# Reading the gathered distance tables one unit further ahead in a disentangled-attention stage

## The reference, cut to what matters

```
pos_k  = (rel_embeddings @ Wk + bk)                          # 128 relative positions, by head
scores = q @ k.T / scale                                     # scale = sqrt(16 * 3)
c2p    = take_along_axis(q @ pos_k.T, clip(rel + 64))        # query against position
p2c    = take_along_axis(k @ pos_k.T, clip(-rel + 64)).T     # key against position
probs  = softmax(scores + (c2p + p2c) / scale)
ctx    = probs @ v
out    = layernorm(ctx @ Wo + bo + hidden) ...
```

## Time and profile before

| | us |
|---|---|
| median of the 3 runs shown | 2644.16 |
| the profiled execution, whole | 2643.83 |
| its span, first to last instruction | 2642.1 |
| stage 1, to the barrier's end | 0 to 157 |
| stage 2, until stage 3 starts | 157 to 1369 |
| stretch between first unit and the last reads of stage 2 | 182 to 1343 |

### The profile page before, as it was taken

How to read it: one execution, slowest core, us unless ns; L and a number is a source line. 1 busy time by engine, 2 the same in 40 slices (tenths; PEclk the granted TensorE clock), 3 DMA queues, 4 the chain that set the end, 5 groups by cost and what they waited for, 6 DMA issues and landing times. The chain is left out here.

```text
span 2642.1 us, 47030 instructions
## 1 busy us (share of the span) xinstructions
PE 1935.7 (73%) x13556; PEld 1436.8 (54%) x13557; DVE 1632.1 (62%) x3986; ACT 998.6 (38%) x2034; POOL 896.3 (34%) x1082
## 2 busy tenths in 40 slices
PE   6867777777777777777759999775623438999962
PEld 3436666665566666666646666543423417887631
DVE  8946666666656666666666455258775794444444
ACT  3445555555555555555523233243201103333100
POOL 3112222222222222223222222037753005555576
PEclk9978899889989899888979999887766558999976
DMA  4579999998999999999952110000000144446544
GB/s 147 184 231 281 281 282 275 270 277 267 288 265 288 269 287 282 272 288 278 291 166 84 48 48 32 1 0 0 1 0 30 37 191 138 153 156 145 121 131 122
DMA packets 289512, 456.38 MB, mean 173 GB/s; under 512 B 38465, under 2 KB 224369, under 8 KB 289297
## 3 DMA queue, kind: packets, MB, share of 16 engines
q1 hardware_dynamic: 272688, 410.29, 50.9%
q0 software_dynamic: 16608, 43.44, 6.7%
HBM read 236.65 MB, written 216.92 MB: 172 GB/s over the span
## 5 line engine op out<-in xcount | busy, mean ns | idle before, releaser
L947 DVE CUSTOM_DVE_ANT_0 probs<-bank,c2p 128x512 f32<-128x512 f32 x512 | 351.7, 687 | 427.6 <-PE bank L844 214.8
L905 ACT ACTIVATE probs<-probs,neg_max 128x512 f32<-128x512 f32 x512 | 371.3, 725 | 68.4 <-DVE neg_max L947 68.1
L920 ACT COPY a_stage<-bank 128x320 f32<-128x320 f32 (+1 forms) x512 | 211.8, 414 | 427.9 <-PE bank L813 417.0
L956 DVE COPY probsT<-bank 128x512 f32<-128x512 f32 x512 | 351.2, 686 | 10.5 <-PE bank L854 9.9
L854 PE MATMUL bank<-ident,probs 128*128 128x128 f32 x2048 | 334.5, 289 | 3.4 <-ACT probs L905 3.3
L825 PE MATMUL bank<-tab,k 96*128 96x320 bf16 (+1 forms) x512 | 164.2, 321 | 187.3 <-DVE b_stage L899 143.3
L854 PEld LDWEIGHTS bank<-ident,probs 128*128 128x128 f32 x2048 | 277.1, 152 | 15.1 <-issue 3.8
L774 POOL COPY end_c2p<-a_stage 128x4 f32<-128x4 f32 (+1 forms) x128 | 24.7, 193 | 745.9 <-ACT a_stage L920 593.1
L2144 POOL DMA_INDIRECT p_x_tile<-y_d,p_token x160 | 152.0, 950 | 283.2 <-POOLq L1845 162.6
L844 PE MATMUL bank<-ident,p2c 128*128 128x128 f32 x1280 | 246.8, 294 | 0.0
L839 PE MATMUL bank<-k,q 96*128 96x384 bf16 (+1 forms) x512 | 166.0, 324 | 101.6 <-DMA p2c<-p2c_d 67.4
(11 more groups left out here) (265 smaller groups left out, 3700.2 us busy)
## 6 DMA issues: line engine op xcount, KB each, us to landing
p2c_d<-b_stage SPq DMA_DIRECT2D x64, 640.0 KB, 4.8
c2p_d<-a_stage SPq DMA_DIRECT2D x64, 640.0 KB
p2c_d<-b_stage SPq DMA_DIRECT2D x64, 576.0 KB, 5.1
c2p_d<-a_stage SPq DMA_DIRECT2D x64, 576.0 KB
p2c<-p2c_d SPq DMA_DIRECT2D x256, 144.0 KB, 4.3
c2p<-c2p_d SPq DMA_DIRECT2D x256, 144.0 KB, 4.1
o_sorted_d<-p_o_pair SPq DMA_DIRECT2D x80, 256.0 KB, 2.3
k<-k_stack_d SPq DMA_DIRECT2D x192, 64.0 KB
```

Source lines behind the costliest of these rows:

```text
L905: act.activation(probs[:, w % 2, j, :], probs[:, w % 2, j, :], ACT.Exp, bias=neg_max[:, w % 2, j:j + 1], scale=-1.0).then_inc(exp_done, 1)
L920: act.copy(staged(a_stage, wa % 2, wa % TPB)[:, j, :], bank[A_BANK][:, 0:width(wa % TPB)]).then_inc(a_copied, 1)
L947: dve.tensor_tensor_reduce(probs[:, w % 2, j, :], bank[S_BANKS[(HB * w + j) % 3]][:], c2p[:, w % 2, j, :], -SCALE, LOWEST, ALU.add, ALU.mi ...
L956: dve.tensor_copy(probsT[:, wp % 2, j], bank[T_BANKS[j % 2]][:].rearrange("p (k q) -> p k q", k=TPB)).then_inc(probsT_copied, 1)
```

## The change

The write leads become 4 and 5, the query side is read back two units ahead (`C2P_LEAD`) and the key side three (`P2C_LEAD`). `p2c` and both HBM tables have eight slots, `c2p` has four, and `probs` is gone: VectorE and ScalarE work in place in `c2p`'s slot. SP waits for the scores of unit n-2 and no longer for the read of a table slot before it writes it again. The prologue has five steps, not four. The quarters of a group's stacks are loaded in the first three steps of each four (two, one, one, none). The values are written to HBM by head in stage 1, with one column of ones (`v_d`), and loaded by SP, one DMA for a head. In `v_h` a tile takes 17 columns, and the matmul still reads 32, the rest of them the next tile's.

```diff
-        c2p_d = dram("c2p_d", [4, P * (B // 2) * TABLE], F32)
-        p2c_d = dram("p2c_d", [4, P * (B // 2) * TABLE], F32)
+        c2p_d = dram("c2p_d", [2 * TPB, P * (B // 2) * TABLE], F32)
+        p2c_d = dram("p2c_d", [2 * TPB, P * (B // 2) * TABLE], F32)
+        v_d = dram("v_d", [H, P, TILES, D + 1], F32)
...
                         if u:
+                            tiles = slice((b - 1) * TPB, (b + 1) * TPB)
+                            sp.wait_ge(v_ones_set, 1)
+                            sp.wait_ge(v_ready, 2 * b + 2)
+                            sp.dma_start(v_d.rearrange("h p t d -> p h t d")[:, :, tiles], v_all[:, :, tiles, :]
+                                         ).then_inc(v_stored, 16)
                             sp.wait_ge(far_split, b // 2 + 1)
...
+                    pool.memset(v_all[:, :, :, D], 1.0).then_inc(v_ones_set, 1)
+                    pool.wait_ge(v_ones_set, 1)
...
-                        dve.tensor_tensor(v_all[:, b * TPB + 2 * j:b * TPB + 2 * j + 2, :],
-                                          bank[V_BANK][:].rearrange("p (s c) -> p s c", s=2), bv_row[:], ALU.add
-                                          ).then_inc(v_ready, 1)
+                        dve.tensor_tensor(v_all[:, :, tiles, 0:D].rearrange("p h s d -> p s h d"),
+                                          bank[V_BANK][:].rearrange("p (s h d) -> p s h d", s=2, h=H),
+                                          bv_row[:].rearrange("p s (h d) -> p s h d", h=H), ALU.add).then_inc(v_ready, 1)
...
-        A_LEAD, B_LEAD = 3, 4
+        A_LEAD, B_LEAD, C2P_LEAD, P2C_LEAD = 4, 5, 2, 3
...
-            v_h = sb(st, "v_h", [P, 2, TILES, MV])
+            v_h = sb(st, "v_h", [P, 2, TILES * (D + 1) + MV - D - 1])
...
-            c2p = sb(st, "c2p", [P, 2, HB, S])
+            c2p = sb(st, "c2p", [P, 4, HB, S])
...
-            p2c = sb(st, "p2c", [P, TPB, HB, NEAR])
-            probs = sb(st, "probs", [P, 2, HB, S])
+            p2c = sb(st, "p2c", [P, 2 * TPB, HB, NEAR])
...
+                    def load_v(h, par):
+                        sp.dma_start(v_h[:, par, 0:TILES * (D + 1)],
+                                     v_d[ds(h, 1)].rearrange("h p t d -> (h p) (t d)")).then_inc(v_loaded[par], 16)
...
                         if is_unit(i, w):
-                            wait_count(sp, scores_made, HB * n)
+                            wait_count(sp, scores_made, HB * (n - 1))
                             apart(sp)
-                        (i2, w2), (i1, w1) = ahead(i, w, 2), ahead(i, w, 1)
+                        (i3, w3), (i2, w2) = ahead(i, w, P2C_LEAD), ahead(i, w, C2P_LEAD)
+                        if is_unit(i3, w3):
+                            kt = w3 % TPB
+                            sp.wait_ge(b_written[w3 % 2], 16 * (BODY // 2 * i3 + w3 // 2 + 1))
+                            apart(sp)
+                            sp.wait_ge(p2c_filled, BODY * i3 + w3 + 1)
+                            read_skewed(p2c_d, w3 % (2 * TPB), kt, p2c[:, w3 % (2 * TPB)], 0, p2c_loaded[kt])
                         if is_unit(i2, w2):
...
-                        if is_unit(i1, w1):
-                            t = w1 % TPB
-                            sp.wait_ge(a_written[w1 % 2], 16 * (BODY // 2 * i1 + w1 // 2 + 1))
-                            apart(sp)
-                            sp.wait_ge(c2p_filled, BODY * i1 + w1 + 1)
-                            read_skewed(c2p_d, w1 % 4, t, c2p[:, w1 % 2], (t - 1) * P, c2p_loaded[w1 % 2])
+                            sp.wait_ge(c2p_filled, BODY * i2 + w2 + 1)
+                            read_skewed(c2p_d, w2 % (2 * TPB), t, c2p[:, w2 % 4], (t - 1) * P, c2p_loaded[w2 % 4])
                         if is_unit(i, w) and is_unit(*ahead(i, w, 2 * TPB)):
                             slot = (w // TPB + 2) % 4
-                            load_quarter(sp, w % TPB, 2 * i + w // 8 + 1, (w // TPB) % 2, slot, group_loaded[slot])
...
+                            for r in ((0, 1), (2,), (3,), ())[w % TPB]:
+                                load_quarter(sp, r, 2 * i + w // 8 + 1, (w // TPB) % 2, slot, group_loaded[slot])
...
+                        if w % 8 == 2 and is_unit(i, w) and is_unit(*ahead(i, w, 6)):
+                            wait_count(sp, pv_made, n - 2)
+                            apart(sp)
+                            load_v(2 * i + w // 8 + 1, 1 - w // 8)
...
-                            wait_count(sp, p2c_loaded[wb % TPB], 64 * (4 * ib + wb // TPB))
...
-                    def copy_v(h, par):
-                        pool.tensor_copy(v_h[:, par, :, 0:D], v_all[:, :, ds(h * D, D)]).then_inc(v_copied, 1)
...
-                            wait_count(pool, scores_made, HB * n)
-                            pool.wait_ge(b_ends_copied, BODY * i2 + w2 + 1)
+                        if is_unit(i3, w3):
+                            t = w3 % TPB
+                            if is_unit(i, w):
+                                wait_count(pool, scores_made, HB * (n - 1))
+                            pool.wait_ge(b_ends_copied, BODY * i3 + w3 + 1)
...
-                            wait_count(pool, scores_added, HB * n)
-                            pool.wait_ge(a_ends_copied, BODY * i1 + w1 + 1)
+                            if is_unit(i, w):
+                                wait_count(pool, probs_transposed, HB * (n - 1))
+                            pool.wait_ge(a_ends_copied, BODY * i2 + w2 + 1)
...
-                    pool.memset(v_h[:, :, :, D:MV], 1.0).then_inc(ones_set, 1)
-                    copy_v(0, 0)
+                    pool.memset(v_h[:, :, TILES * (D + 1):], 0.0).then_inc(pad_set, 1)
...
-                                                probs[:, w % 2, j, kt * P:(kt + 1) * P], ident[:])
+                                                c2p[:, w % 4, j, kt * P:(kt + 1) * P], ident[:])
...
-                                pe.wait_ge(v_copied, 2 * i + g // 2 + 1)
+                                pe.wait_ge(v_loaded[g // 2], 16 * (i + 1))
...
-                                    dve.wait_ge(c2p_loaded[w % 2], 64 * (8 * i + w // 2 + 1))
+                                    dve.wait_ge(c2p_loaded[w % 4], 64 * (4 * i + w // 4 + 1))
```

## The result

The changed kernel took 2689.6 us (median of 4 runs, 2687.4 to 2694.8) against 2647.6 us for the one before (4 runs, 2642.0 to 2651.9): ratio 1.0163, interval 1.0135 to 1.0191. The forecast was 2593 us in a range of 2553 to 2640, so the sign was wrong as well as the size. In the profiled execution the span is 2686.5 us against 2642.1. Where the runs of a kernel fall into a faster and a slower state, as those of e14_stacks_by_act further down do, its ratio takes the faster ones alone.

A forecast was written before the change was run, and what follows sets the result against it. The prediction took the DMA engines to bound the attention stage, at share 0.94 and 278 GB/s. 2643.8 less 51 us there, plus 0 for the start and end, gave 2593 us, range 2553 to 2640.

The forecast's parts named there:

- The order of the group's quarters: Attention stage: bunching stack loads only shifts SP's issue time between steps; taken as nothing, up to 30 us for the range.
- SP's and POOL's waits: Attention stage: the dropped or moved waits of SP and POOL, and POOL's 16 fewer copies, change nothing; 0 us.
- One step more between read and use: Attention stage: earlier reads remove the query-side wait, 182.2 us, and most of the key-side 61.3 us; DMA queue is late next.
- The cap by the DMA engines: Attention stage: 327 MB at 300 GB/s plus 20 us of loop returns, 1110 us against 1161, a gain of 51.
- C: Attention stage: SP's own issue order is the clock; gain of 0 to 25 us, 2619 to 2644; chance 0.15.
- A: Attention stage, the forecast case: waits go and the DMA engines cap the gain; 2575 to 2615 us; chance 0.62.
- rival B: Attention stage: DMA ceiling higher than seen; at 312 GB/s a gain of 93 us, 2551; far end compute-bound; chance 0.12.
- Values by DMA: Attention stage: loading values by DMA adds 4.2 MB, making 327 MB in all, priced at 300 GB/s.
- Stage 1 and the prologue: Stage 1 +2 us, fifth prologue step +3, smaller first memset -1, last unit's read wait -4; together 0.
- Rival D: Attention stage: the DMA queue is full already, so the kernel gets slower; 2661 to 2671 us; chance 0.11.

The follow-up runs named there:

- e14_stacks_by_act: e13_act_two_bodies with the key stacks issued by ScalarE too; 0.9479 of the kernel before, from two of its four runs.
- e1_k_alone: Changed kernel with separate semaphores for key and query stacks, so the key-side product waits for the key stacks only; 0.9900 of the kernel before.
- e2_quarters_early: Changed kernel with the stack quarters loaded one a step, starting two steps earlier; 0.9899 of the kernel before.
- e9_both: The mended kernel: changed kernel with separate key and query stack semaphores and quarters one a step, two steps earlier; 0.9872 of the kernel before.
- e12_before_by_act: Kernel before with the query stacks' loads issued by ScalarE instead of SP, one step earlier; 0.9936 of the kernel before.
- e8_query_side_alone: Kernel before with query side read two units ahead into four slots, quarters two steps earlier, key side and values unchanged; 0.9944 of the kernel before.
- e10_queries_by_act: e9_both with the query stacks' loads issued by ScalarE at the end of its step instead of SP; 0.9626 of the kernel before.
- e4_before_bunched: Kernel before with only the quarters' order changed to two, one, one, none, leads as before; 1.0033 of the kernel before.
- after_again: The changed kernel unaltered, timed again on another chip beside e9_both; 1.0169 of the kernel before.
- e6_two_bodies: e9_both with two bodies in each pass of the hardware loop, two returns for five; 0.9820 of the kernel before.
- e13_act_two_bodies: e9_both with query stacks issued by ScalarE and two bodies in each loop pass; 0.9549 of the kernel before, 2525.3 us.

## Why the prediction was wrong

**The step that failed** is "The order of the group's quarters", together with "SP's and POOL's waits". It priced the new order by what its issues cost SP and took nothing for it, with 30 us as the bound. It never asked when the stack is wanted. The key-side product of a group's first unit is made `B_LEAD` units ahead; with `B_LEAD` 5 it is made in the step w % 4 = 3 of the group before, and the last quarter of the query stack is issued in the step just before that, w % 4 = 2, behind that step's eight reads. In the kernel before the distance was one step as well (quarter issued in step 3, wanted in step 0), and the prediction had its sign in hand: TensorE's 25.6 us for `q_stack`, at most 2.1 us at a time. It was read as a small wait. In its place the runs showed 255.3 us in pieces of 8.5: by the reading above, a wait with a cover, VectorE's wait for the query side, which the change takes away. The price was 71 to 78 us (e1_k_alone, e2_quarters_early, e9_both), more than all the gain that was forecast.

**"One step more between read and use"** was right in itself: 182.2 us fell to 2.3, and in the mended kernels the waits went to the staging buffers as foreseen. e12_before_by_act agrees that the lead held the kernel before. e8_query_side_alone adds that it takes both leads: the query side's alone gave 0.6%.

**The cap by the DMA engines** was too generous for this change and is not the cap that it was taken for. The prediction had a gain of 51 us in the stage, at a share of nearly 1.00 but for the returns. From the first sum to the last, e9_both takes 1137 us where the kernel before takes 1172: a gain of 35. Its share stayed at 0.96, with SP almost never waiting, so the limit of one queue that issues everything came first; the prediction gave that rival, C, a chance of 0.15 by the earlier trace rows, and took it and A as alternatives. The rate of 300 GB/s at full share is about right (309 at 1.02, 317 at 1.03), but a share of 1.00 is no ceiling even over a whole stage: e10_queries_by_act makes the same transfers in a stretch of 1069 us (180.4 to 1249.1), 103 less than before and more than rival B's 93.

**Values by DMA** were put at the bytes' price, 4.2 MB / 300 GB/s = 14 us, with about 2 us in stage 1. Alone they cost 0.41% or 11 us (6 to 16): the sum agrees, but the trace of that run shows the attention stage as long as before, so the agreement may be luck.

**The quarters' order as an issue cost** was taken as 0 of 0 to 30 us; e4_before_bunched measured 0.33% or 9 us.

**Stage 1 and the prologue.** Stage 2 started at 159.37 instead of 157.25, +2.1 for the forecast 2, in this timeline line of the changed kernel beside the earlier trace rows:

```profile
159.37 0.12 POOL L804 MEMSET v_h<- 128x30 f32 x1 [58.00 <-POOLq L85]
```

The additions of stage 1 kept their 685 ns, as taken:

```profile
L500 DVE TENSOR_TENSOR p_v<-bank,p_bv_row x16: 682/685/693, 43.1 to 151.0; 128x512 f32<-128x512 f32 x16
```

The first unit came 6.8 us later; 2.1 of them are stage 1, so the prologue cost 4.7 for the forecast 3 less 1. (In after_again it came 4.2 us later; a single trace gives this to some 3 us.) The last unit's wait of 3.98 us went, as forecast; its first sum now waits for nothing:

```profile
1391.85 0.68 DVE L963 CUSTOM_DVE_ANT_0 c2p<-bank,c2p 128x512 f32<-128x512 f32 x1
```

**Rival D** named the right sign by the wrong mechanism: the queue was not full, and the mended kernels move 291 to 317 GB/s. The rule of the Trainium skill that it leaned on ("DMA: Bandwidth & Descriptors", section "Issuing engines are not separate DMA queues": all DMAs end up on the same 16 engines) is no bar to a gain here, since e10_queries_by_act raised the rate from 291 to 309 GB/s by issuing the same loads from another engine.

**What stays open.** Why the mended kernel gains from a second queue (above). And within the changed kernel the DMA share is 0.85 to 0.91 in most windows of a group and not only at the stall. That this follows from the late quarter is shown, since both cures bring it to 0.95 to 0.96; by which route each hundredth is lost (SP waiting for copies, SP's small loads while compute runs at 6.9 us a unit, the slower clock after a stall) was not separated.

## What to carry to other kernels

Before you remove a wait, list every other load and buffer that is asked for at the same distance: a wait of 2 us may be a late transfer under a cover, and it comes out at full length. When one instruction is moved ahead by a step, go through all that it waits for, not only the buffer that the move is about, and move those issues too. And where one queue issues everything, price a small load by its turn in that queue and not only by its bytes: the same 11.8 MB issued from a second engine took 2.5% off the mended kernel, and 0.6% off the one before, which waited for something else.

## What the runs showed of the hardware

The stage ran at 278 GB/s with share 0.94, 291 with 0.96, 309 with 1.02 and 317 with 1.03, with nearly the same transfers: 296 to 308 GB/s for each full share. The share of 0.96, with one queue issuing everything, was not what full engines give: with the same transfers and a second queue it was 1.02. TensorE's granted clock was 0.50 in the window of 6 us in which it did nothing, stayed there for the first 4 us of work after it, and was 1.00 again from 610; over the stretch it was 0.85 with the stalls and 0.90 without. The loop's return costs about 4 us of the 16 engines each time by the trace before; three returns fewer were worth 14 us in e6_two_bodies, whose interval reaches that of e9_both, and 20 us in e13_act_two_bodies.
